# Values of two heads projected in one rounded pass, and weights asked for when their buffer has been split

## The reference

```python
b, s, _ = x.shape
q = split_heads(x @ Wq)
k = split_heads(x @ Wk)
v = split_heads(x @ Wv)
q = _apply_rope(q, cos, sin)
k = _apply_rope(k, cos, sin)
scores = jnp.einsum('bhqd,bhkd->bhqk', q, k) * scale
attn = jax.nn.softmax(jnp.where(causal[None, None], NEG_INF, scores), axis=-1)
ctx = jnp.einsum('bhqk,bhkd->bhqd', attn, v)
...
return ctx @ Wo
```

## Time and profile before

| | us |
|---|---|
| runs | 1116.43, 1115.67, 1110.38; median 1115.67 |
| the profiled execution | 1113.77 |
| its span, from the first to the last instruction | 1111.9 |
| TensorE busy in the span | 1009.6 (91%) |
| VectorE, ScalarE, GpSimd busy | 691.5, 590.2, 462.4 |

### The profile page before, as it was taken

How to read it: one execution, slowest core, us unless ns; L and a number is a source line. 1 busy time by engine, 2 the same in 40 slices (tenths; PEclk the granted TensorE clock), 3 DMA queues, 4 the chain that set the end, 5 groups by cost and what they waited for, 6 DMA issues and landing times. The chain is left out here.

```text
span 1111.9 us, 18673 instructions
## 1 busy us (share of the span) xinstructions
PE 1009.6 (91%) x5954; PEld 819.2 (74%) x5954; DVE 691.5 (62%) x2084; ACT 590.2 (53%) x1632; POOL 462.4 (42%) x481
## 2 busy tenths in 40 slices
PE   8999999998995699759899999988878889999995
PEld 5889898987873599637678888865445568777784
DVE  5766666663675356546755663136787557888785
ACT  3565666565221355436666773047874555555653
POOL 5778767760377444366111110010137214443322
PEclk9999999999996799979999999988998989999998
DMA  6631011100011699624301101001003011122001
GB/s 213 248 141 60 25 30 29 30 1 1 1 56 54 204 352 335 224 83 139 98 25 62 30 21 38 1 22 51 2 1 116 0 57 57 57 66 89 18 1 39
DMA packets 83495, 85.59 MB, mean 77 GB/s; under 512 B 8545, under 2 KB 75943, under 8 KB 83280
## 3 DMA queue, kind: packets, MB, share of 16 engines
q1 hardware_dynamic: 79056, 75.39, 21.1%
q0 software_dynamic: 3072, 7.34, 2.2%
q10 hardware_dynamic: 1280, 1.77, 0.5%
HBM read 63.36 MB, written 22.02 MB: 77 GB/s over the span
## 5 line engine op out<-in xcount | busy, mean ns | idle before, releaser
L565 POOL TENSOR_TENSOR a_qk<-h,a_by_sin 128x512 f32<-128x512 f32 x64 | 81.7, 1277 | 5.0
L348 DVE CUSTOM_DVE_ANT_0 h<-a_score_ps,mask_bf 128x128 f32<-128x128 f32 (+1 forms) x128 | 40.8, 356 | 59.3 <-PE a_score_ps L341 59.3
L1281 POOL TENSOR_TENSOR a_w_l<-a_w,a_w_h 128x256 fp32r<-128x256 f32 x30 | 22.0, 735 | 110.7 <-ACT a_w_h L1474 110.5
L354 ACT ACTIVATE y_moe<-y_moe,a_nmax 128x128 f32<-128x128 f32 x64 | 25.7, 402 | 76.0 <-DVE a_nmax L348 76.0
L448 PEld LDWEIGHTS a_proj_ps<-a_w,xT 128*128 128x128 f32 x512 | 62.0, 192 | 3.1 <-issue 1.2
L1020 POOL TENSOR_TENSOR e_w_l<-e_w,e_w_h 128x512 fp32r<-128x512 f32 x32 | 41.0, 1281 | 53.2 <-ACT e_w_h L1088 53.2
L448 PE MATMUL a_proj_ps<-a_w,xT 128*128 128x128 f32 x512 | 62.4, 275 | 0.4 <-DVE hT L506 0.4
L76 PE MATMUL a_proj_ps<-a_x_l,a_w_h 128*128 128x512 f32 x128 | 57.3, 448 | 0.3 <-POOL a_w_l L570 0.3
L744 PE MATMUL t_y_ps<-wo,attnT 128*128 128x256 f32 x256 | 57.6, 381 | 0.0
L2536 POOL TENSOR_TENSOR m_up_l<-m_up_w,m_up_h 128x1024 fp32r<-128x1024 f32 x8 | 19.5, 2432 | 90.1 <-ACT m_up_h L2508 90.1
L1521 PE MATMUL p_y_ps<-wo,attnT 128*128 128x256 f32 x256 | 55.5, 379 | 0.8 <-PEq L1253 0.8
(11 more groups left out here) (443 smaller groups left out, 3380.0 us busy)
## 6 DMA issues: line engine op xcount, KB each, us to landing
slots<-zeros SPq DMA_DIRECT2D x4, 2048.0 KB, 7.4
e_rows<-slots SPq DMA_DIRECT2D x32, 256.0 KB, 4.7
e_w<-in_L_ffn_w_dram SPq DMA_DIRECT2D x32, 256.0 KB, 4.8
out_slots<-e_out SPq DMA_DIRECT2D x32, 256.0 KB, 4.2
e_w<-in_L_ffn_w_dram SPq DMA_DIRECT2D x32, 128.0 KB, 4.3
a_w<-in_L_attn_w_q_dram SPq DMA_DIRECT2D x32, 128.0 KB, 2.3
m_up_w<-in_up_dram SPq DMA_DIRECT2D x8, 512.0 KB, 3.8
a_w<-in_L_attn_Wq_dram SPq DMA_DIRECT2D x16, 128.0 KB, 2.3
```

What stands on the lines that cost most here:

```text
L348: done = dve.tensor_tensor_reduce(self.probs[:, b, cells], self.score_ps[:, r, cells], self.k.mask_bf[:, cells], -1.0, 3e38, ALU.add, ALU. ...
L354: act.activation(self.probs[:, b, 0:P], self.probs[:, b, 0:P], ACT.Exp, bias=self.nmax[:, b, 0:1], scale=-1.0, accum_out=self.total[:, b, ...
L565: pool.tensor_tensor(qk[:, par, 0 if what == "q" else 1, half * HALF:(half + 1) * HALF], by_cos[:, r, :], by_sin[:, r2, :], ALU.add).then_ ...
```

## The change

- Values are projected for a group of two heads at once (VG = 2, 8 groups) with `product`: 128 tokens stationary, 256 columns of Wv moving, three passes. A value chunk is now two token tiles by 256 columns, so 12 matmuls of 128x256; there are four chunks a group, again 32 in all.
- Wv has a landing buffer wv of its own, for one group, and split parts wv_h, wv_l for two groups, which lie where x is loaded. The split is ScalarE's (batch 1 of each odd head) and VectorE's (batch 3 of each odd head); the first group's low part is GpSimd's.
- Before the first head's scores eight chunks are projected and not six: q0, k0, v0, q1, k1, v1, v2, v3. Later chunks stand where they stood; the last two heads have no value chunks beside them.
- load(h) brings Wq and Wk alone and waits until the low part of head h - 2 has been made. load_v(g) waits until the low part of group g - 1 has been made. x is loaded after the last value chunk. Odd groups' projected values are kept in the memory of xT.

```diff
-                    at_least(sp, v_proj, 2 * (h - 2) + 2)
-                    for n, name in enumerate(("L0_attn_Wq", "L0_attn_Wk", "L0_attn_Wv")):
+                    if h == 3:
+                        sp.wait_ge(w1_low, 2)
+                    elif h >= 2:
+                        sp.wait_ge(w_low, 2 * max(h - 3, 0) + 2)
+                    for n, name in enumerate(("L0_attn_Wq", "L0_attn_Wk")):
...
+                def load_v(g):
+                    if g:
+                        low_of(sp, g - 1)
+                    sp.dma_start(wv[:, :, :], I["L0_attn_Wv"][:, g * VG * HD:(g + 1) * VG * HD
+                                                              ].rearrange("(c p) d -> p c d", p=P)).then_inc(wv_in, 16)
                 load(0, 0)
+                load_v(0)
                 load(1, 1)
+                load_v(1)
                 load_rest(sp, k, I)
                 load(2, 0)
-                load_tail(sp, k, I)
+                load_v(2)
+                load_wo(sp, k, I)
                 rows = SLOTS // P // ZERO_DMAS
                 for h in range(3, H):
                     load(h, h % 2)
+                    if h % VG and (h + 3) // VG < GROUPS_V:
+                        load_v((h + 3) // VG)
...
+                sp.wait_ge(v_proj, B * GROUPS_V)
+                load_x(sp, k, I)
...
+        OPENING = [("q", 0, 0), ("k", 0, 0), ("v", 0, 0), ("q", 0, 1), ("k", 0, 1), ("v", 0, 1), ("v", 0, 2), ("v", 0, 3)]
...
+            values = [("v", g, 2 * (h % VG) + i) for i in range(2)] if g < GROUPS_V else [None, None]
+            jobs = {0: [("q", h + 1, 0), ("k", h + 1, 0)], 1: [values[0], ("q", h + 1, 1)],
+                    2: [("k", h + 1, 1), values[1]], 3: []}[b]
...
+                        for t in range(QT):
+                            cells = slice((QT * i + t) * P, (QT * i + t + 1) * P)
+                            for kc in range(DC):
+                                last = product(pe, out[:, t * VG * HD:(t + 1) * VG * HD],
+                                               (x_h[:, kc, cells], x_l[:, kc, cells]),
+                                               (wv_h[:, of % 2, kc, :], wv_l[:, of % 2, kc, :]), kc == 0, kc == DC - 1)
...
+                def cut_values(g):
+                    dve.wait_ge(wv_high, g + 1)
+                    dve.tensor_tensor(wv_l[:, g % 2], wv[:, :, :], wv_h[:, g % 2], ALU.subtract).then_inc(wv_low, 1)
...
                         if n >= at.TURN:
                             at.copy_turned(dve, n - at.TURN, (b - at.TURN) % B)
+                        if b == B - 1 and par and (h + 3) // VG < GROUPS_V:
+                            cut_values((h + 3) // VG)
...
+                def keep_v(g, j):
+                    act.wait_ge(v_proj, B * g + j + 1)
+                    at_least(act, at.mixed, B * (VG * (g - 1) - 1) + j + 1)
...
                 def cut_high(h, pair, par):
-                    act.wait_ge(w_in[par], 48 * (pair + 1))
-                    at_least(act, v_proj, 2 * (h - 1))
+                    act.wait_ge(w_in[par], 32 * (pair + 1))
+                    at_least(act, qk_proj, 4 * (h - 1))
...
+                def cut_values(g):
+                    act.wait_ge(wv_in, 16 * (g + 1))
+                    at_least(act, v_proj, B * (g - 1))
+                    act.activation(wv_h[:, g % 2], wv[:, :, :], ACT.Copy).then_inc(wv_high, 1)
```

More of the change, by code:

```diff
@@ L431, in project @@
                     if what == "v":
-                        pe.wait_ge(w_in[par], 48 * (pair + 1))
+                        pe.wait_ge(v_kept, B * of + i + 1)
                     else:
[L434 to L440, removed]
@@ L441, in project @@
-                    if prev in NQK:
-                        at_least(pe, rot_in, 4 * prev_h + NQK[prev])
-                    else:
[L444 to L454, removed]
-                            last = product(pe, proj_ps[:, c % 2, :], w_p[:, par, PIECE[what], kc, :],
-                                           (x_h[:, kc, tokens], x_l[:, kc, tokens]), kc == 0, kc == DC - 1)
-                        last.then_inc(qk_proj, 1)
+                        pe.wait_ge(rot_in, 4 * of + COUNT[what, i])
@@ L475, in emit @@
                                   lambda i, j: qk[:, par, 1, b * S + i:b * S + j])
-                        if not last:
-                            for c in BESIDE[b]:
-                                project(h + 1, pair + par, 1 - par, c)
+                        for job in beside(h, b):
+                            project(job)
                         if b >= at.TURN or not first:
@@ L494, in _, with rotate_in @@
             def _(dve):
-                def rotate_in(h, c):
-                    what, half = CHUNKS[c]
-                    count = 4 * h + NQK[c]
-                    r = NQK[c] - 1
+                def rotate_in(job):
+                    what, h, half = job
+                    count = 4 * h + COUNT[what, half]
+                    r = COUNT[what, half] - 1
                     dve.wait_ge(qk_proj, count)
@@ L580, in emit @@
                     if not last:
-                        for c in NQK:
-                            rotate(h + 1, c, 1 - par)
+                        for what, half in COUNT:
+                            rotate(h + 1, what, half, 1 - par)
                 heads(emit)
@@ L603, in _ @@
                         cut_high(0, 0, 0)
+                        cut_values(0)
                 cut_high(1, 0, 1)
-                for c in NV:
-                    keep_v(0, 0, c)
+                keep_v(0, 0)
+                keep_v(0, 1)
+                cut_values(1)
+                keep_v(0, 2)
+                keep_v(0, 3)
                 def emit(h, pair, par, first, last, ahead):
@@ L613, in emit @@
                             cut_high(h + 2, pair + 1, par)
+                        if b == 1 and par and (h + 3) // VG < GROUPS_V:
+                            cut_values((h + 3) // VG)
                         if n:
@@ L617, in emit @@
                             at.keep_mixed_act(act, n - at.KEEP, b, h - 1)
-                        if not last:
-                            for c in BESIDE[b]:
-                                if c in NV:
-                                    at_least(act, at.mixed, 4 * h - 2 + 2 * CHUNKS[c][1])
-                                    keep_v(h + 1, 1 - par, c)
+                        for job in beside(h, b):
+                            if job[0] == "v":
+                                keep_v(job[1], job[2])
                 heads(emit)
```

111 lines of the change are left out of this document (78 added, 33 removed).

## The result

The changed kernel takes 1117.74 us (median of 20 runs, 1112.95 to 1121.58) where the kernel before takes 1113.76 (20 runs, 1110.01 to 1116.43). The ratio is 1.0036, with a 95% interval of 1.0024 to 1.0048. So it is slower by 4.0 us: within the range of 1103.5 to 1121 and within the 0.5% that the forecast called no change.

A forecast was written before the change was run, and what follows sets the result against it. TensorE, busy for 91% of the span and full in the first attention, was taken as the bound. Terms -10.9 + 0.4 + 8.8 + 0.2 + 1.6 = +0.1 us against 1113.77 gave about 1114 us, range 1103.5 to 1121.

The forecast's parts named there:

- value chunks: First attention: 32 chunks, each 1.44 us as 12 rounded matmuls where 1.78 before; -10.9 us.
- opening: Start of the kernel: first split waits for fewer transfers, but cut_values delays the second half of x; +0.4 us.
- loads of heads 4 and 6: Their weights queue behind load_v and a 2 MB clearing, so ScalarE, then TensorE, wait in heads 2 and 4; +8.8 us.
- loads of heads 8, 10, 12: Their weights queue behind load_v alone, with 0.4 us of cover; +0.2 us in all, at most 1 each.
- clock: After TensorE's waits in heads 2 and 4 the granted clock may fall to half; 0.8 us each, +1.6 us.
- behind the stage: After the first attention, past 267 us: no change claimed; 0.
- Splits at zero: Added splits on ScalarE, VectorE and GpSimd in the first attention are covered by idle time; zero by itself.
- The faster one (1103.7): Rival: loads of heads 4 and 6 come in time and cost like those of 8 to 12; 1103.7 us, chance 0.22.
- The slower one (1120.3): Rival: heads 2 and 4 wait 5 us each and half clock costs 3.4 us each; 1120.3 us, chance 0.15.
- the third: Rival: value pass of 256 columns is no gain, chunks cost 1.78 us again and waits remain; 1125 us, chance 0.03.

The follow-up runs named there:

- the kernel before with the early request: Kernel before, with query and key weights asked for once their landing buffer is split and Wv as before: 1113.39 us against 1113.52, ratio 0.999.
- filler kernel: Changed kernel plus four unused matmuls on zeros on TensorE ahead of the turn of batch 1 in heads 2 and 4: 1116.56 us, ratio 1.0034 against before.
- halves: Changed kernel with the clearing in eight transfers of 1 MB, not four of 2 MB: 1114.87 us, ratio 1.0017.
- the kernel with the loads in time: Changed kernel with load_v issued behind the even head's query and key weights on SyncE's queue, not ahead of them: 1104.87 us against 1113.1, ratio 0.9935.
- the kernel with the later split: Changed kernel with ScalarE's weight split in batch 2, not batch 0, and GpSimd's part behind the rotation of k0: 1105.73 us, ratio 0.9942.
- the kernel before made late: Kernel before, with the first and third clearing and the loads of heads 4 and 6 held back to the end of heads 1 and 3: 1123.63 us, 1.0081.

## Why the prediction was right and wrong

For the large terms the mechanism was the predicted one: the place on the queue, ScalarE's wait in heads 2 and 4 (5.86 and 7.37 us, predicted 5), TensorE's at the turn, a clock below 1.00. Two things were not as predicted: ScalarE waits in heads 6, 8 and 10 as well (2.81, 2.50 and 1.66), where no such wait was to be, so heads 6 and 8 are not shorter; and the opening had a second cause. The sum was 3.2 us too low, by the sizes of four terms, above all the loads of heads 4 and 6:

| term | predicted | measured |
|---|---|---|
| value chunks | -10.9 | 32 x (1.78 - 1.41) = -11.8 |
| opening | +0.4 | (23.44 - 20.56) - (4 x 1.41 - 2 x 1.78) = +0.8, and 0.4 more in head 0 |
| loads of heads 4 and 6 | +8.8 | 5.44 + 5.33 = +10.8 |
| loads of heads 8, 10, 12 | +0.2 | 0.79 + 0.68 = +1.5 |
| clock | +1.6 | 0.71 + 1.70 = +2.4 |
| behind the stage | 0 | -0.7 |
| sum, profiled executions | +0.1 | +3.3 |

- **Value chunks: right.** 0.118 us a matmul, as 0.12 in the earlier trace rows. The Trainium skill's rule that the prediction set beside it (TensorE: Matmul & The Clock Gate, Back-to-back issue gap) would give 0.109; the rows stay above it in this stage too. (The gain that the prediction set beside it is 32 x (1.78 - 12 x 0.109) = 15.1, not 15.2 us.)
- **Loads of heads 4 and 6: the step that failed is the landing of the clearing.** Issues came at +1.1, +1.5, +2.3 and +2.9 after the head's first scores, as counted. The clearing was taken at 7.1 us and took 8.4 and 8.3, so Wk landed at +10.7 and +10.6, not +9.8. All that followed was right: the line above gives 9.8 - 5.29 = 4.5 for the predicted landing, and the prediction had 4.4. Rows of before would have warned, had I read all four clearings, which all have nothing right behind them. They took 7.6, 7.1, 7.0 and, in the DMA view of the kernel before for the last of them:

```profile
slots<-zeros SPq DMA_DIRECT2D x1, 2048.0 KB, 8.9
```

  I built on a short one, and on one with nothing behind it. The clearings of 2 MB that had loads right behind them, and no other transfer of 2 MB still under way, took 7.8 to 8.7 us in every kernel, in the kernel before with the early request too (8.7, 7.8, 7.8). Whether the loads behind are what lengthens them was not tried by itself. The term's upper bound, 5.6 a head, named this case and held it.
- **Loads of heads 8 and 10: the cover of 0.4 us was right, the landing was not.** Wk behind 256 KB took 4.0, 3.4 and 2.8 us, I counted 2.7. It landed at +6.1, +6.0 and +5.1, and the limit is +5.29, so two of three lose. I had put a bound of 1 on each and inside it the most favourable value, where a cover of 0.4 us behind an uncertain landing calls for the middle.
- **Clock: the right mechanism, undersized by 0.8.** After the filler kernel, 3.4 us at the 1.2 GHz level cost 0.7, and 6.8 us cost 1.7. The price is less than half the time at that level. In part that is because TensorE at full clock waits 0.77 at k1 for keep_v anyway (so in the filler kernel and with halves), as the prediction said of the first 2.7 us, and because 1.05 of the 6.8 us passed before TensorE resumed. These two would leave 0.9 and 2.1 us; the rest is not traced. The clock fell at both waits. The Trainium skill's warning (TensorE: Matmul & The Clock Gate, HAM oscillation), that waits for DMA let the array restart cold, holds here for the second; at the first TensorE had already run for 0.75 us at 1.00. It is worth 2.4 of 1117 us.
- **Opening: the reason was right, and a second one was missing.** From ScalarE's first split of weights to the first value chunk it is 13.77 - 9.23 = 4.54 us in the kernel before and 14.58 - 8.86 = 5.72 in after, 1.18 more. Of these 0.69 are the later rounding of x behind cut_values, which the prediction named (up to 0.8). The other 0.57 stood in no term: VectorE's pair takes 2.36 and not 1.79, beside GpSimd's split of values. With ScalarE's order alone changed the stretch takes 5.59, the one cost traded for the other; with GpSimd's split held back as well it takes 13.39 - 8.85 = 4.54 again. Against it stands that the first split began 0.37 earlier, the gain from two transfers instead of three (predicted about 0.5). But in the six kernels with after's opening it began anywhere from 8.62 to 9.63, so one execution can't give the +0.8 to better than half a us. The 0.4 in head 0 is not traced.
- **Splits at zero: right only where nothing long stands behind them.** In after they cost nothing. With the loads mended, the one on VectorE ahead of the squares costs 0.6 once.
- **Rivals.** The faster one (1103.7) supposed loads in time. They were not, but its price was good: the kernel with the loads in time measured 1104.87. The slower one (1120.3) had waits of 5 us a head and a fall of the clock at both; without the clock the two heads lost 5.4 and 5.3 and the clock did fall at both, but it counted 3.4 us for each fall and they cost 2.4 in all. Its mechanism came nearer than the forecast's. The experiment for the value pass answers the third: a head with it is shorter by 0.74.

## What to carry to other kernels

A wait on an in-order DMA queue delays all that stands behind it, and a large transfer behind that wait makes it costly (heads 6 and 8 of after lost 0.7 to 0.8 us without one, heads 2 and 4 5.3 to 5.4 with one, before the clock): a change that moves a request on the queue is to be read by what comes behind it, and here one line of order was worth 13 us, more than the 11.8 us of arithmetic that the change saved. When a term is the lateness of one operation, find from the trace at what point its user begins to wait (here 5.29 us into the head); beyond it each microsecond of a late landing costs one, so read every landing of that kind, not one. Operations of VectorE and GpSimd that each read two tensors are to be kept apart in time as if they were one engine's.

## What the runs showed of the hardware

- **On SyncE's queue small transfers behind a large one land with it, not 2.4 us after their issue.** Wk of 128 KB: 2.4 us with Wq alone ahead, 2.8 to 4.0 behind 256 KB, 4.4 to 5.1 behind 1 MB more, 7.8 behind 2 MB more (6.5 to 9.1 in the other kernels). Wk lands 0.7 to 1.1 us after the clearing, once 2.4 after (filler, head 4); Wq, issued between them, lands within 0.7 us of it on either side, once 1.35 ahead. The issues behind it get longer as well: 1.09 us for Wk in head 2 of after, where the earlier trace rows have 0.37 to 0.58.
- **VectorE and GpSimd with two inputs each slow one another, and the rows fit one of them waiting out the other's instruction.** A subtraction of 128x512 on VectorE took 0.68 alone, and on average 0.9, 1.2 and 1.5 each in the pairs of 1.79, 2.36 and 2.92 us, the more of GpSimd's time they met. In the kernel with the later split, GpSimd's addition began at 53.54 and VectorE's squares ended at 52.23 + 3.38 = 55.61; the addition took 3.20. The Trainium skill (SBUF — State Buffer, Who interferes with whom) calls the pair of ports that both engines use an exclusive lock. An estimate by it: the later one waits for 2.07 us and then takes its 1.28, 3.35 in all. The row agrees to 0.15 us. So do the pairs: a pair alone takes 1.29 us (at 6.99 in after), and the instruction of GpSimd that they met ended at 11.16 in the kernel before and at 12.04 in after. That makes 12.45 and 13.33 for their ends, and they ended at 12.30 and 13.19. The prediction had read the pair of 1.79 in the earlier trace rows as a price and not as a sign of this.
- **How long the clock stays down doesn't follow the idle time in a plain way.** In after, 3.83 us of idle TensorE brought 3.4 us at the 1.2 GHz level and 4.04 brought 6.8; with ScalarE's order changed, 3.62 brought 3.4 and 4.19 brought 6.8; in the kernel before made late, 2.92 and 4.33 brought 3.4 each. In the kernel with halves, 1.1 to 1.5 us brought no fall. What decides was not tried.
